# Second attention: the negated row maxima are copied into the score banks by ScalarE and VectorE in turn, where a 128-row product put them

## The chip, the cores and the metric

The kernel runs on one core of one Trainium2 chip. The metric is the device time of one execution in microseconds (us), the median of three runs. Engines are named as in the profile: PE is TensorE, PEld its weight loads, DVE is VectorE, ACT is ScalarE, POOL is GpSimd.

## The reference

The input `x` has 2048 rows of width 128. Four blocks follow one another, each on the layer-normalised output of the last and added to it: a first attention with 16 heads of width 64, a feed-forward block, a second attention, and the same feed-forward block again. The change is in the second attention. It has 8 heads of width 128, rotary positions and a causal mask:

```python
q = jnp.einsum('btm,mhd->bthd', x, w_aq)
k = jnp.einsum('btm,mhd->bthd', x, w_ak)
v = jnp.einsum('btm,mhd->bthd', x, w_av)
q = _rope(q)
k = _rope(k)
s = jnp.einsum('bihd,bjhd->bhij', q, k) / D_HEAD
...
s = s - jnp.asarray(INF_APPROX, x.dtype) * mask      # mask: i < j
p = jax.nn.softmax(s, axis=-1)
o = jnp.einsum('bhij,bjhd->bihd', p, v)
r = jnp.einsum('bihd,hdm->bim', o, w_ao)
```

The inputs are spread so widely that the softmax needs the maximum of each row, and products in one half-precision part are not exact enough.

## The kernel before, in words

Each engine has a program of its own, written out in order, and the engines meet only at semaphores: an instruction that waits holds back everything behind it on its engine.

**Tiles.** A head of the second attention has 4 units, one for each block of 512 queries (`qb` 0 to 3). A unit walks over the keys 128 at a time, so that `qb` has 4, 8, 12 or 16 steps, 40 in a head and 320 in all (`PLACES_B`, with the running number `g`). The last four steps of a unit lie on the diagonal, and their tiles are 512, 384, 256 and 128 queries wide (`c0` is where they begin). All units have an even number of steps, so `g` is even where the step is.

**A score tile.** Scores stand transposed, keys on the partitions and queries along the row. The two banks `SB[0]` and `SB[1]` take the tiles in turn. `scores_b(g)` (L1820) puts a tile there with four products of 128x512: minus the maximum of each query, lifted by a constant, comes first, as `row_units` times `MROW` (L1832). Then come, on the diagonal, the mask (L1835) and always K high times Q high, K low times Q high and K high times Q low (L1837 to L1839), since each operand is split into a high and a low half-precision part. ACT takes the exponential of the bank twice, in single precision into `PRB` (L911) and in half precision into `PAH` (L913); POOL subtracts the one from the other into `PAL` (L704). Two steps later (`LAG_B`) PE multiplies both parts by the values, in two halves (`pv_b`, L1859 to L1863, 12 products of about 128 columns for a full tile).

**The ring.** Everything else that PE makes goes through three banks, `RING3B`, as numbered items: PE writes an item (`ring_put`), DVE takes it (`ring_taken`), and item n may be written once item n-3 is taken (`claim`). The table `PLAN_B` says which items each step has, beside the tile and its values. A digit is a product of scores for the maxima of a later unit (`max_b`, L1773), of which DVE takes the maximum (L1094). P is a projection of Q or K for the next head (L1748 to L1750); DVE takes it in three instructions for the rotary positions (L1314 to L1316). V is a part of the next head's values; ACT copies it (L872), then DVE subtracts (L1335). T and O turn and project the output of the unit before. An r with a digit is the item "rows".

```python
PLAN_B = [
    ["2 2", "2", "2 T", "P O"],
    ["2 V", "2", "2 V", "2 2 2", "2 2", "T", "r2 3 P", "O"],
    ["3 3 3", "3", "3 3", "3", "3 3", "3 3 P T", "3", "3", "3 3", "P", "r3", "O"],
    ["0", "0 0", "P", "0", "P", "", "r0 1 T", "", "1 V", "1 P", "1", "1 1 1", "P", "", "1 V O", "r1"],
]
```

PE's order in a step is: the score tile, the first item, one half of the values product, the second item, the other half, the remaining items, with T and O always last. The last head has no items for a next one, so its P, V, 0 and 1 fall away.

**The rows item.** When the last maximum of a unit is taken, DVE makes `negmax` (L1097). PE turns it (L1540), and DVE writes it lifted and spread over four rows into `MROW` (L1116), which serves all tiles of the unit.

Of the kernel before, what the change touches and what calls it, by code (L numbers as in the profile page):

```python
# [35 lines left out]
F16 = mybir.dt.float16  # L36
I32 = mybir.dt.int32
ALU = mybir.AluOpType
# [3 lines left out]
P = 128  # L42
# [3 lines left out]
BLK = 512  # L46
# [226 lines left out]
def build(nc, x, adaptive_scale, Wq, bq, Wk, bk, Wv, bv, Wo, bo, gamma, beta,  # L273
          w_aq, w_ak, w_av, w_ao, W1, b1, W2, b2, rope_cos, rope_sin, out):
    ctx = ExitStack()
    with ctx:
# [84 lines left out]
        row_units = sb("row_units", [P, P], F16)  # L361
        MROW = sb("MROW", [P, 2, BLK], F16)
# [117 lines left out]
        def phase(n):  # L480
# [9 lines left out]
            s.pv = sem(f"pv_{n}")  # L490
            s.fourth_taken = sem(f"fourth_taken_{n}")
# [3 lines left out]
        sa, sbb = phase("a"), phase("b")  # L495

# [78 lines left out]
        def _(pool):  # L575
# [20 lines left out]
            pool.memset(MROW[:, :, :], 0.0)  # L596
            link(pool.memset(row_units[:, :], 0.0))
            pool.memset(row_units[0:BT, :], ROW_UNIT)
# [121 lines left out]
        def _(act):  # L720
# [183 lines left out]
            for g, (it, ul, step) in enumerate(PLACES_B):  # L904
# [37 lines left out]
        def _(dve):  # L942
# [147 lines left out]
            def take_max(s, bank, item, qt, c, width, chunks, last, unit):  # L1090


                dve.wait_ge(s.ring_put, item + 1)
                dve.reduce_max(maxes[:, qt, c:c + 1], bank[:, 0:width], X_AXIS).then_inc(s.ring_taken, 1)  # L1094
                if last:
                    dve.wait_ge(s.ring_taken, item + 1)
                    dve.tensor_reduce(negmax[:, :], maxes[:, :, 0:chunks], X_AXIS, ALU.max, negate=True  # L1097
                                      ).then_inc(s.max_ready, 1)
                    dve.wait_ge(s.max_ready, unit + 1)
# [281 lines left out]
            for i in range(BT):  # L1381
                n = 5 * BLOCKS + i
                take_max(sbb, RING3B[n % 3], n, i, 0, (i + 1) * P, 1, i == BT - 1, 0)
            take_rows(sbb, RING3B[ROWS_LEAD_B % 3], ROWS_LEAD_B, MROW[0:BT, 0, :], lifts_b[0:BT, 0:1])
            for i, (qt, c) in enumerate(max_items_b(1)):
                n = ROWS_LEAD_B + 1 + i
                take_max(sbb, RING3B[n % 3], n, qt, c, BLK if c < 1 else (qt + 1) * P, 2, i == 2 * BT - 1, 1)
            take_rows(sbb, RING3B[(LEAD_B - 1) % 3], LEAD_B - 1, MROW[0:BT, 1, :], lifts_b[0:BT, 0:1])
# [10 lines left out]
            for g, (it, ul, step) in enumerate(PLACES_B):  # L1399
# [7 lines left out]
                if place in (5, 6):  # L1407
                    normalise(4 * BLOCKS + place - 5, place - 5)
                if step == LAG_B and g > step:
                    normalise_b((ul - 1) % UNITS_B, g - step)  # L1410
                for n, item in ITEMS_B[g]:
                    bank = RING3B[n % 3]
                    if item[0] == "max":
# [3 lines left out]
                        take_max(sbb, bank, n, i, c, BLK if c < target else (i + 1) * P, target + 1,  # L1417
                                 item[2] == len(todo) - 1, it * UNITS_B + target_unit(ul, target))
                    elif item[0] == "rows":
                        h = head + (item[1] < qb)  # L1420
                        take_rows(sbb, bank, n, MROW[0:BT, item[1] % 2, :], lifts_b[0:BT, h:h + 1])
# [26 lines left out]
        def _(pe):  # L1448
# [87 lines left out]
            def rows(s, bank, item, unit):  # L1536

                claim(s, item)
                pe.wait_ge(s.max_ready, unit + 1)
                pe.transpose(bank[0:BT, 0:P], negmax[:, :], ident[:, :]).then_inc(s.ring_put, 1)  # L1540
# [277 lines left out]
            rows(sbb, RING3B[ROWS_LEAD_B % 3], ROWS_LEAD_B, 0)  # L1818
            pe.wait_ge(ones_set, 2)

            def scores_b(g):
# [3 lines left out]
                if step == 0:  # L1825
# [154 lines left out]
```

## Time and profile before

| what | value |
|---|---|
| median of 3 runs | 1928.9 us (1926.85 to 1929.04) |
| span of the profiled execution | 1927.3 us |
| PE busy | 1854.3 us, 96% |
| POOL busy | 1597.5 us, 83% |
| ACT busy | 1548.5 us, 80% |
| DVE busy | 1443.6 us, 75% |
| second attention, score tiles | 1277 to 1889 us |

The profiled execution is known by its span, from the first to the last instruction; the runs' times hold what lies around it too, and their median is 1.6 us above it. Busy time counts an instruction from its start to its end, and neighbours can overlap: PE's products have modelled ends. The pitch, from one start to the next, is what a product costs PE, and the timelines below show it.

### The profile page before, as it was taken

The page shows a single profiled execution, that of the slowest core. Times are in us where ns is not written, and L with a number is a line of the kernel's source. Part 1 is how long each engine was busy: PE and PEld are TensorE (multiplying, and loading weights), DVE is VectorE, ACT ScalarE, POOL GpSimd, SP SyncE. Part 2 cuts the span into 40 slices and gives each one's busy share as a digit, 9 for nine tenths or more (in the row PEclk, how much of TensorE's full clock was granted, in tenths as well). Part 3 has the DMA queues.
Part 4 walks back from the last instruction along what each step waited for, and adds up shares of the span by engine and source line. Part 5 has one row for each costly group of instructions (what it writes and reads, how often), then busy time and mean ns, then how long its engine had stood idle before and what let it go on. Part 6 is the DMA issues. An engine that isn't in the chain of part 4 may idle for free.

```text
span 1927.3 us, 55726 instructions
## 1 busy us (share of the span) xinstructions
PE 1854.3 (96%) x23471; PEld 1256.4 (65%) x23471; DVE 1443.6 (75%) x2647; ACT 1548.5 (80%) x1921; POOL 1597.5 (83%) x1025
## 2 busy tenths in 40 slices
PE   4899999999999999999999998779999999999998
PEld 3566666666666666666666665547777777767766
DVE  7798878878878878878878875566767767767652
ACT  4799999999999999999999999646666666666664
POOL 3899999999999999999999999358688787787752
PEclk8999999999999999999999999889999999999999
DMA  6101100100100100100100100100000000000000
GB/s 148 35 11 26 34 15 22 35 17 20 35 19 18 35 19 18 35 19 17 35 23 14 35 2 2 55 1 2 2 1 2 2 2 2 2 1 1 2 2 23
DMA packets 45034, 37.96 MB, mean 20 GB/s; under 512 B 8304, under 2 KB 44144, under 8 KB 44528
## 3 DMA queue, kind: packets, MB, share of 16 engines
q1 hardware_dynamic: 44304, 34.00, 7.0%
q8 instruction: 186, 3.05, 0.7%
q10 hardware_dynamic: 480, 0.39, 0.1%
q14 instruction: 64, 0.52, 0.1%
HBM read 8.15 MB, written 1.05 MB: 5 GB/s over the span
## 4 chain that ended last, share of the span: by engine, by line
PE 87%; DVE 4%; POOL 3%; issue 3%; ACT 2%; DMA 0%; SPq 0%; POOLq 0%; DVEq 0%; ACTq 0%
PE ST L1639 11%; PE ST L1640 11%; PE RING L1520 7%; PE OO L1601 6%; PE OO L1603 6%; PE OO L1600 6%; PE OO L1520 4%; PE ST L1832 3%; PE ST L1838 3%; PE ST L1837 3%; PE ST L1839 3%; POOL PBUF L704 2%; PE OO L1859 2%; PE OO L1861 2%; PE OO L1863 2%
## 5 line engine op out<-in xcount | busy, mean ns | idle before, releaser
L620 POOL TENSOR_TENSOR PAB<-PR,PAB 128x1024 f16<-128x1024 f32 x342 | 724.3, 2134 | 42.3 <-ACT PAB L799 42.2
L799 ACT ACTIVATE PAB<-ST,exp_scale 128x1024 f16<-128x1024 f32 x512 | 567.6, 1109 | 0.0
L1104 DVE TENSOR_REDUCE maxes<-RING 128x1 f32<-128x512 f32 x661 | 439.6, 684 | 122.6 <-PE RING L1520 118.2
L1600 PE MATMUL OO<-VP,PAB 128*128 128x66 f16 x4096 | 446.6, 192 | 2.9 <-POOL PAB L620 2.9
L1601 PE MATMUL OO<-VP,PAB 128*128 128x64 f16 x4096 | 447.1, 193 | 0.0
L1603 PE MATMUL OO<-VP,PAB 128*128 128x66 f16 x4096 | 445.1, 192 | 0.0
L797 ACT ACTIVATE PR<-ST,exp_scale 128x1024 f32<-128x1024 f32 x342 | 381.9, 1117 | 64.7 <-PE ST L1640 61.8
L1600 PEld LDWEIGHTS OO<-VP,PAB 128*128 128x128 f16 x4096 | 380.2, 96 | 78.3 <-issue 15.5
L1601 PEld LDWEIGHTS OO<-VP,PAB 128*128 128x128 f16 x4096 | 377.0, 97 | 60.6
L1639 PE MATMUL ST<-QL,KH 128*128 128x512 f16 x1024 | 388.6, 380 | 2.0 <-DVE QH L1116 1.0
L1640 PE MATMUL ST<-QH,KL 128*128 128x512 f16 x1024 | 388.8, 380 | 0.0
L620 POOL TENSOR_TENSOR PAB<-VF,PAB 128x1024 f16<-128x1024 f32 x170 | 362.6, 2133 | 26.9 <-ACT PAB L799 26.9
L1603 PEld LDWEIGHTS OO<-VP,PAB 128*128 128x128 f16 x4096 | 378.0, 98 | 0.0
L1104 DVE TENSOR_REDUCE maxes<-OO 128x1 f32<-128x512 f32 x363 | 248.4, 684 | 67.9 <-PE OO L1520 64.3
L704 POOL TENSOR_TENSOR PBUF<-PR,PBUF 128x512 f16<-128x512 f32 (+1 forms) x214 | 216.0, 1013 | 98.8 <-ACT PBUF L913 92.8
L911 ACT ACTIVATE PR<-ST,exp_scale_b 128x512 f32<-128x512 f32 (+1 forms) x214 | 133.5, 624 | 136.2 <-PE ST L1839 132.1
L1520 PE MATMUL RING<-KH,QL 128*128 128x512 f16 x661 | 228.5, 381 | 6.5 <-DMA QH<-HS 3.1
L797 ACT ACTIVATE VF<-ST,exp_scale 128x1024 f32<-128x1024 f32 x170 | 189.7, 1116 | 33.8 <-PE ST L1640 32.1
L913 ACT ACTIVATE PBUF<-ST,exp_scale_b 128x512 f16<-128x512 f32 (+1 forms) x320 | 198.1, 619 | 0.0
L1094 DVE TENSOR_REDUCE maxes<-RING 128x1 f32<-128x512 f32 (+3 forms) x216 | 128.9, 611 | 54.7 <-PE RING L1773 53.6
L1859 PE MATMUL OO<-PAB,PBUF 128*128 128x130 f16 x768 | 150.9, 220 | 2.8 <-POOL PBUF L704 2.7
L1861 PE MATMUL OO<-PAB,PBUF 128*128 128x128 f16 x768 | 151.2, 221 | 0.0
(319 smaller groups left out, 4027.8 us busy)
## 6 DMA issues: line engine op xcount, KB each, us to landing
KH<-HS SPq DMA_DIRECT2D x124, 64.0 KB, 2.0
QL<-HS SPq DMA_DIRECT2D x64, 64.0 KB, 2.0
QL<-LS SPq DMA_DIRECT2D x64, 64.0 KB, 2.0
QH<-HS SPq DMA_DIRECT2D x64, 64.0 KB, 2.0
KL<-LS SPq DMA_DIRECT2D x62, 64.0 KB, 2.0
X<-in_L_attn_a_x SPq DMA_DIRECT2D x4, 256.0 KB, 4.2
SHARED<-in_rope_cos SPq DMA_DIRECT2D x1, 1024.0 KB, 5.2
SHARED<-in_rope_sin SPq DMA_DIRECT2D x1, 1024.0 KB, 7.3
```

The costliest lines, as they stand in the source:

```text
L620: pool.tensor_tensor(PB[:, s, :], PRA[g % PR_SLOTS], PA[:, s, :], ALU.subtract).then_inc(p_low_ready, 1)
L704: pool.tensor_tensor(PAL[:, g % SLOTS_B, c0:BLK], PRB[g % PR_SLOTS_B][:, c0:BLK], PAH[:, g % SLOTS_B, c0:BLK], ALU.subtract).then_inc(p_lo ...
L797: act.activation(PRA[g % PR_SLOTS], ST[step % 2][:, :], ACT.Exp, scale=scale)
L799: act.activation(PA[:, step % SLOTS_A, :], ST[step % 2][:, :], ACT.Exp, scale=scale).then_inc(sa.exps, 1)
L913: act.activation(PAH[:, g % SLOTS_B, c0:BLK], SB[g % 2][:, c0:BLK], ACT.Exp, scale=scale).then_inc(sbb.exps, 1)
L1104: dve.reduce_max(maxes[:, i // BLOCKS, i % BLOCKS:i % BLOCKS + 1], bank[:, :], X_AXIS).then_inc(sa.ring_taken, 1)
L1520: pe.matmul(RING3[item % 3][:, :], QL16[head % 2][:, at:at + P], KH16[head % 2][:, c * BLK:(c + 1) * BLK], start=True, stop=True).then_inc ...
L1600: pe.matmul(o, high, v[:, 0:V2_AT], start=(m == 0 and qt == 0), stop=False, skip_group_check=True)
L1601: pe.matmul(o[:, V1_AT:V2_AT], high, v[:, V2_AT:VCOL], start=False, stop=False, skip_group_check=True)
L1603: ins = pe.matmul(o, low, v[:, 0:V2_AT], start=False, stop=(m == TILES - 1), skip_group_check=True)
L1639: pe.matmul(tile, KH16[hs][:, keys], QL16[hs][:, q], start=True, stop=False)
L1640: ins = pe.matmul(tile, KL16[hs][:, keys], QH16[hs][:, q], start=False, stop=True)
```

## The change

`row_units`, `MROW` and the product L1832 go. In their place:

- Behind `negmax`, DVE makes `negmax16` (lifted, scaled, half precision), 128x4.
- The rows item is now `seed_b`: four products of 128x128 (`spread`) put minus the maxima, repeated over all partitions, into a ring bank. DVE copies the whole bank into `SEED`, 128x512 in single precision (`take_seed_b`). `SEED` has two places, by the parity of `qb`.
- Before PE writes a score tile, the seed is copied from `SEED` into its bank, and PE's products add to it (none of them starts the sum). For even tiles ACT copies, behind its two instructions of tile g, the seed of tile g+2. For odd tiles DVE copies, in step g (even), the seed of tile g+1: behind the take of the step's first ring item, before the second.
- ACT's half-precision instruction no longer takes the exponential of the bank: it copies `PRB`, and waits for the first to be finished. The bank is free after the first exponential.
- Tiles 0 and 1 get their seed by `spread` straight into the bank.

```diff
 # ScalarE
-                act.activation(PRB[g % PR_SLOTS_B][:, c0:BLK], SB[g % 2][:, c0:BLK], ACT.Exp, scale=scale)
+                p = PRB[g % PR_SLOTS_B][:, c0:BLK]
+                act.activation(p, SB[g % 2][:, c0:BLK], ACT.Exp, scale=scale).then_inc(sbb.first_exps, 1)
                 wait(act, sbb.pv, g - SLOTS_B + 1)
-                act.activation(PAH[:, g % SLOTS_B, c0:BLK], SB[g % 2][:, c0:BLK], ACT.Exp, scale=scale
-                               ).then_inc(sbb.exps, 1)
+                act.wait_ge(sbb.first_exps, g + 1)
+                act.activation(PAH[:, g % SLOTS_B, c0:BLK], p, ACT.Copy).then_inc(sbb.exps, 1)
+                if g % 2 == 0 and g + 2 < len(PLACES_B):
+                    tile, seed, taken = seed_of(g + 2)
+                    act.wait_ge(sbb.ring_taken, taken)
+                    act.activation(tile, seed, ACT.Copy).then_inc(sbb.seeds_act, 1)
 # VectorE
+                    link(dve.tensor_reduce(negmax[:, :], maxes[:, :, 0:chunks], X_AXIS, ALU.max, negate=True))
+                    dve.tensor_scalar(negmax16[:, :], negmax[:, :], lifts_b[:, head:head + 1], 1.0 / ROW_UNIT,
+                                      ALU.add, ALU.mult).then_inc(sbb.max_ready, 1)
...
+            def take_seed_b(bank, item, unit):
+
+                dve.wait_ge(sbb.ring_put, item + 1)
+                dve.tensor_copy(SEED[:, unit % 2, :], bank[:, :]).then_inc(sbb.ring_taken, 1)
+
+            def seed_scores(t):
+
+                tile, seed, taken = seed_of(t)
+                dve.wait_ge(sbb.first_exps, t - 1)
+                dve.wait_ge(sbb.ring_taken, taken)
+                dve.tensor_copy(tile, seed).then_inc(sbb.seeds_dve, 1)
...
+                seeds_next = g and g % 2 == 0 and g + 1 < len(PLACES_B)
...
-                for n, item in ITEMS_B[g]:
+                for place, (n, item) in enumerate(ITEMS_B[g]):
                     bank = RING3B[n % 3]
+                    if place == 1 and seeds_next:
+                        seed_scores(g + 1)
...
+                if seeds_next and len(ITEMS_B[g]) < 2:
+                    seed_scores(g + 1)
 # TensorE
+            def spread(bank):
+
+                for i in range(BT):
+                    ins = pe.matmul(bank[:, i * P:(i + 1) * P], negmax16[:, i:i + 1].broadcast_to((P, P)),
+                                    mask_ident[:, :], start=(i == 0), stop=True, skip_group_check=True)
+                return ins
...
-                if step == 0:
-                    pe.wait_ge(sbb.ring_taken, ROWS_OF_B[it * UNITS_B + ul] + 1)
-                wait(pe, sbb.exps, g - 1)
+                if g < 2:
+                    spread(SB[g])
+                else:
+                    pe.wait_ge((sbb.seeds_act, sbb.seeds_dve)[g % 2], g // 2)
...
-                pe.matmul(tile, row_units[:, :], MROW[:, qb % 2, c0:BLK], start=True, stop=False,
-                          skip_group_check=True)
```

The first place is VectorE's order before, in the fifth head, last unit, steps 2 to 6. F and PR are the targets of a projection's take, maxes those of a maximum's:

```order
L1327 TENSOR_TENSOR AB<-OO,rden 128x384
L1314 TENSOR_TENSOR F<-RING,SHARED 128x512 [waits operands_ready_b,ring_put_b]
L1315 TENSOR_TENSOR PR<-RING,SHARED 64x512
L1316 TENSOR_TENSOR PR<-RING,SHARED 64x512
L1094 TENSOR_REDUCE maxes<-RING 128x1 [waits ring_put_b]
L1097 TENSOR_REDUCE negmax<-maxes 128x4 [waits ring_taken_b]
L1314 TENSOR_TENSOR F<-ST,SHARED 128x512 [waits operands_ready_b,ring_put_b,max_ready_b]
L1315 TENSOR_TENSOR PR<-ST,SHARED 64x512
L1316 TENSOR_TENSOR PR<-ST,SHARED 64x512
L1116 SCALAR_TENSOR_TENSOR MROW<-RING,lifts_b,rowmask 4x512 [waits ring_put_b]
```

The same place after the change, with ST<-SEED for a seed that is copied into a score bank:

```order
L1340 TENSOR_TENSOR F<-RING,SHARED 128x512 [waits operands_ready_b,ring_put_b]
L1341 TENSOR_TENSOR PR<-RING,SHARED 64x512
L1342 TENSOR_TENSOR PR<-RING,SHARED 64x512
L1125 COPY ST<-SEED 128x512 [waits ring_taken_b,first_exps_b]
L1106 TENSOR_REDUCE maxes<-RING 128x1 [waits ring_put_b]
L1110 TENSOR_REDUCE negmax<-maxes 128x4 [waits ring_taken_b]
L1111 TENSOR_SCALAR negmax<-negmax,lifts_b 128x4 [waits chain]
L1340 TENSOR_TENSOR F<-ST,SHARED 128x512 [waits operands_ready_b,ring_put_b,max_ready_b]
L1341 TENSOR_TENSOR PR<-ST,SHARED 64x512
L1342 TENSOR_TENSOR PR<-ST,SHARED 64x512
L1125 COPY ST<-SEED 128x512 [waits ring_taken_b,first_exps_b]
L1118 COPY SEED<-RING 128x512 [waits ring_put_b]
```

A seed copy now stands behind each of the two projections' takes of the even steps 2 and 4; `MROW` has become the copy of a whole bank.

The second place is TensorE's order before, in the same unit, from the last values product of step 4 into step 5. ST<-MROW opens the score tile:

```order
L1863 MATMUL ST<-PAB,PBUF 128x130
L1832 MATMUL ST<-MROW,row_units 128x512 [waits exps_b]
L1837 MATMUL ST<-QH_0,KH_0 128x512
L1838 MATMUL ST<-QH_0,KL_0 128x512
L1839 MATMUL ST<-QL_0,KH_0 128x512
L1859 MATMUL OO<-PAB,PBUF 128x130 [waits p_low_ready_b]
```

And after the change:

```order
L1899 MATMUL ST<-PAB,PBUF 128x130
L1873 MATMUL ST<-QH_0,KH_0 128x512 [waits seeds_dve_b]
L1874 MATMUL ST<-QH_0,KL_0 128x512
L1875 MATMUL ST<-QL_0,KH_0 128x512
L1895 MATMUL OO<-PAB,PBUF 128x130 [waits p_low_ready_b]
```

The tile has one product less, and its first one waits for VectorE's seed copy in place of ScalarE's exponentials of two tiles earlier.

## Rows read from the trace of the kernel before

**Rows 1.** Stretches: us; PE, PEld, DVE, ACT, POOL busy (count); granted clock; DMA.

```profile
1588.00:1664.00 76.00, 75.73 (x765) 54.49 (x764) 54.62 (x101) 51.29 (x94) 60.01 (x60) 1.00 0.01 2
1816.00:1890.00 74.00, 70.06 (x689) 49.90 (x686) 36.11 (x96) 50.07 (x87) 43.05 (x44) 0.98 0.01 2
1250.00:1270.00 20.00, 15.44 (x117) 9.96 (x116) 13.70 (x31) 8.75 (x18) 14.55 (x13) 1.00 0.00 1
1270.00:1276.00 6.00, 2.89 (x26) 1.44 (x23) 3.65 (x8) 3.40 (x5) 4.41 (x5) 0.77 0.00 0
```

**Rows 2.** Waits in the fifth head: us in total, times, longest.

```profile
ACT PR L911 <- PE ST L1839: 15.8, 18, 1.8
...
PE OO L1859 <- POOL PBUF L704: 0.3, 1, 0.3
```

**Rows 3.** Timeline, TensorE, last unit, steps 4 to 6: start, length, instruction.

```profile
1639.73 0.38 PE L1832 MATMUL ST<-MROW,row_units 128*128 128x512 f16 x1
1639.94 0.38 PE L1837 MATMUL ST<-QH,KH 128*128 128x512 f16 x1
...
1641.03 0.38 PE L1750 MATMUL ST<-XNT,WHB 128*128 128x512 f16 x1
1641.24 0.22 PE L1859 MATMUL OO<-PAB,PBUF 128*128 128x130 f16 x1
...
1641.93 0.38 PE L1832 MATMUL ST<-MROW,row_units 128*128 128x512 f16 x1
...
1644.33 0.27 PE L1540 MATMUL RING<-ident,negmax 128*4 128x128 f32 x1
1644.44 0.22 PE L1859 MATMUL OO<-PAB,PBUF 128*128 128x130 f16 x1
```

**Rows 4.** Timeline, VectorE, the last instruction of that projection's take.

```profile
1642.91 0.68 DVE L1316 TENSOR_TENSOR PR<-ST,SHARED 64x512 f32<-64x512 f32 x1
```

**Rows 5.** Timeline, TensorE, third unit, steps 4 to 7.

```profile
1618.13 0.38 PE L1773 MATMUL ST<-KH,QH 128*128 128x512 f16 x1
...
1619.25 0.38 PE L1832 MATMUL ST<-MROW,row_units 128*128 128x512 f16 x1
...
1624.07 0.38 PE L1832 MATMUL ST<-MROW,row_units 128*128 128x512 f16 x1
```

**Rows 6.** Timeline, VectorE, the same steps.

```profile
1618.55 0.69 DVE L1094 TENSOR_REDUCE maxes<-ST 128x1 f32<-128x512 f32 x1 [1.34 <-PE ST L1773]
1619.16 0.68 DVE L1094 TENSOR_REDUCE maxes<-RING 128x1 f32<-128x512 f32 x1
...
1624.86 0.68 DVE L1094 TENSOR_REDUCE maxes<-ST 128x1 f32<-128x512 f32 x1
```

**Rows 7.** Timeline, a claim that VectorE's take ends, at the first tiles.

```profile
1280.52 0.69 DVE L1094 TENSOR_REDUCE maxes<-RING 128x1 f32<-128x512 f32 x1 [3.68 <-PE RING L1773]
...
1281.27 0.10 PEld L1772 LDWEIGHTS RING<-later_keys,mask_ident 128*128 128x128 f16 x1 [0.79 <-DVE maxes L1094]
```

**Rows 8.** VectorE by line and shape: count, busy us, mean ns, idle before.

```profile
L1274 DVE TENSOR_TENSOR X<-X,XN 128x512 f32<-128x512 f32 x4 | 4.1, 1023 | 2.5 <-POOL XN L659 2.5
L1397 DVE COPY XNT<-RING 128x512 f32<-128x512 f32 x1 | 0.7, 692 | 1.1 <-PE RING L1873 1.1
L998 DVE TENSOR_SCALAR mask_ident<-ident 128x128 f16<-128x128 f32 x1 | 0.2, 220 | 0.0
L1097 DVE TENSOR_REDUCE negmax<-maxes 128x4 f32<-128x4 f32 x8 | 1.3, 158 | 0.3
```

**Rows 9.** ScalarE by line and shape.

```profile
L911 ACT ACTIVATE PR<-ST,exp_scale_b 128x512 f32<-128x512 f32 x150 | 103.2, 688 | 104.0 <-PE ST L1839 101.0 <-POOL PBUF L704 2.2
L866 ACT ACTIVATE KH<-F 128x512 f16<-128x512 f32 x30 | 18.9, 628 | 0.7 <-POOL F L681 0.6
L732 ACT ACTIVATE XNT<-OO 128x512 f32<-128x512 f32 x4 | 2.3, 584 | 2.3 <-PE OO L1452 2.3
```

**Rows 10.** GpSimd by line and shape.

```profile
L704 POOL TENSOR_TENSOR PBUF<-PR,PBUF 128x512 f16<-128x512 f32 x150 | 173.4, 1158 | 81.6 <-ACT PBUF L913 78.0 <-PE ST L1863 2.7
```

More of the change, by code:

```diff
@@ L360, in build @@
         later_keys_t = sb("later_keys_t", [P, P], F16)
-        row_units = sb("row_units", [P, P], F16)
-        MROW = sb("MROW", [P, 2, BLK], F16)
+        negmax16 = sb("negmax16", [P, BT], F16)
+        SEED = sb("SEED", [P, 2, BLK])
         wqk_raw = RAW[:, 0:HA * P].rearrange("p (h c) -> p h c", c=P)
@@ L490, in phase @@
             s.pv = sem(f"pv_{n}")
+            s.seeds_act = sem(f"seeds_act_{n}")
+            s.seeds_dve = sem(f"seeds_dve_{n}")
+            s.first_exps = sem(f"first_exps_{n}")
             s.fourth_taken = sem(f"fourth_taken_{n}")
@@ L495, in build, with seed_of @@
         sa, sbb = phase("a"), phase("b")
+        def seed_of(t):
+            it, ul, step = PLACES_B[t]
+            qb = ul % BLOCKS
+            c0 = max(0, step - BT * qb) * P
+            return SB[t % 2][:, c0:BLK], SEED[:, qb % 2, c0:BLK], ROWS_OF_B[it * UNITS_B + ul] + 1
         def wait(eng, s, value):
@@ L595, in _ @@
                                fill=1.0 / ROW_UNIT, base=0, pattern=[[-1, BT], [0, P]], channel_multiplier=1).then_inc(consts, 1)
-            pool.memset(MROW[:, :, :], 0.0)
-            link(pool.memset(row_units[:, :], 0.0))
-            pool.memset(row_units[0:BT, :], ROW_UNIT)
             pool.wait_ge(zeros_set, 1)
@@ L1416, in _ @@
                         i, c = todo[item[2]]
-                        take_max(sbb, bank, n, i, c, BLK if c < target else (i + 1) * P, target + 1,
+                        take_max_b(bank, n, i, c, BLK if c < target else (i + 1) * P, target + 1,
                                  item[2] == len(todo) - 1, it * UNITS_B + target_unit(ul, target))
                     elif item[0] == "rows":
-                        h = head + (item[1] < qb)
-                        take_rows(sbb, bank, n, MROW[0:BT, item[1] % 2, :], lifts_b[0:BT, h:h + 1])
+                        take_seed_b(bank, n, item[1])
                     elif item[0] == "project":
@@ L1534, in total_b, with seed_b @@
                           ).then_inc(sa.ring_put, 1)
[L1536 to L1540, printed above, removed]
+            def spread(bank):
[3 more added lines that the diff above has]
+                return ins
+            def seed_b(bank, item, unit):
+                claim(sbb, item)
+                pe.wait_ge(sbb.max_ready, unit + 1)
+                spread(bank).then_inc(sbb.ring_put, 1)
             def turned(s, bank, item, src, units_done):
@@ L1817, in _ @@
                 max_b(0, 0, i, 0, RING3B[n % 3], n, 0)
-            rows(sbb, RING3B[ROWS_LEAD_B % 3], ROWS_LEAD_B, 0)
+            seed_b(RING3B[ROWS_LEAD_B % 3], ROWS_LEAD_B, 0)
             pe.wait_ge(ones_set, 2)
@@ L1888, in ring_item_b @@
                 elif item[0] == "rows":
-                    rows(sbb, bank, n, it * UNITS_B + target_unit(ul, item[1]))
+                    seed_b(bank, n, it * UNITS_B + target_unit(ul, item[1]))
                 elif item[0] == "project":
@@ L1908, in _ @@
                         max_b(0, 1, qt, c, RING3B[n % 3], n, 0)
-                    rows(sbb, RING3B[(LEAD_B - 1) % 3], LEAD_B - 1, 1)
+                    seed_b(RING3B[(LEAD_B - 1) % 3], LEAD_B - 1, 1)
                 elif g > 1:
```

21 lines of the change are left out of this document (10 added, 11 removed).

## The prediction, made before the change was run

> **What bounds the kernel now.** I read the stretches first, for the share of each engine in one head of the second attention, then the waits there, then the timelines of PE and DVE side by side. The fifth head takes 76.0 us and PE is busy for 75.7 of them at the full clock, 2.4 GHz; POOL has 60.0, DVE 54.6 and ACT 51.3 [rows 1]. The waits agree: ACT waits for PE 18 times in front of L911 alone, while PE waits once for POOL, 0.3 us [rows 2]. So this part lasts as long as PE's products do, and the others have 16 to 25 us of slack per head. The reader is to see two more things. First, PE writes the next tile whenever it gets there: the product L1832 at 1641.93 follows the values products without a gap, though DVE is at that time still at work on the projection that PE ended at 1641.24 [rows 3], until 1642.91 + 0.68 = 1643.59 [rows 4]. Second, this is allowed because three ring banks stand between the two engines, and because nothing that a score tile needs comes from DVE in the same step.
>
> **What the change removes on PE.** A product of 512 columns costs its pitch, 1639.94 - 1639.73 = 0.215 us when read over several (the row has 0.21) [rows 3]. A head has 24 tiles off the diagonal and 16 on it with a mean of 320 columns, which together are 34 full widths: 34 x 0.215 = 7.3 us per head, 58.4 us for eight. The turn of the maxima (0.11 us, from L1540 at 1644.33 to L1859 at 1644.44 [rows 3]) becomes four products of 128 columns, 4 x 0.055 = 0.22 us, so 32 x 0.11 = 3.5 us come back. Before the first tile PE no longer waits for `MROW`: about 1 us less. PE's own work falls by 58.4 - 3.5 + 1 = 55.9 us. If the new seeds always came in time, that would be the gain.
>
> **The seeds of odd tiles: a new wait of PE for DVE.** In each even step g, DVE copies the seed of tile g+1 only behind the take of that step's first ring item, and PE reaches tile g+1 right behind step g. DVE's path starts at the item itself. For one maximum: the product starts at 1618.13, DVE at 1618.55 [rows 5, 6], 0.42 us later; its take has a pitch of 0.61 us (1618.55 to 1619.16) [rows 6]; then comes the copy, and then the way to PE, 0.06 us (a take ends at 1280.52 + 0.69 = 1281.21, PE's waiting load starts at 1281.27) [rows 7]. No row has a DVE copy from SBUF to PSUM. The nearest is the same instruction the other way, 0.692 us (L1397) [rows 8]; from below there is L998, 128 columns from SBUF to SBUF in 0.220 us against 0.158 us for 4 columns, which stretched to 512 gives 0.16 + 4 x 0.06 = 0.40 us; from above L1274 with two SBUF sources, 1.02 us [rows 8]. I take 0.69, since one side is in PSUM as in the nearest row. Copies of 384 and 128 columns I take at 0.55 and 0.28. So tile g+1 can start at 1618.55 + 0.61 + 0.69 + 0.06 = 1619.91, and PE was there at 1619.25 [rows 5]: a stall of 0.66 us, in a step that even had a second item behind the first.
>
> A rule of the Trainium skill bears on this price. "VectorE: DVE Perf Modes", section "Mode 2×_2P — use both read ports for one tensor", says that a single-source fp32 copy runs at two elements a cycle only where source and destination are in SBUF. By it the seed copy stays at the full 0.69 us, and the low end of 0.40 us doesn't come; the rows agree as far as they go, since the copy out of PSUM has the single rate and the narrow one inside SBUF looks faster.
>
> The same reading, step by step through the fifth head (end of DVE's take of the first item as the trace has it, plus copy and way, minus PE's start of the next tile), gives four classes of the 20 even steps:
> - The first item is a projection: 3 steps (units' steps qb3 2, 4, 12). Step 4: 1643.59 + 0.75 = 1644.34 against 1641.93 [rows 3, 4], 2.41 us. The others 2.36 and 2.22: 7.0 us.
> - A maximum or rows item that stands on DVE behind a projection of the step before: 3 steps (qb2 6 and 10, qb3 10). qb2 6: the take starts at 1624.86, so 1624.86 + 0.61 + 0.75 = 1626.22 against 1624.07 [rows 5, 6], 2.15 us. The others 1.5 and 1.4: 5.05 us.
> - One item alone, or little behind it: 5 steps, 0.74 to 1.0 us, together 4.4 us.
> - Two items, or items of middle length: 6 steps, 0.3 to 0.66 us, together 2.9 us. In the other 3 a V, P or O behind the first item covers the copy.
>
> Sum 19.3 us per head. These stalls add up, since each lies between an item that PE has just written and the next tile: time lost earlier moves both ends alike. DVE isn't full: 54.6 + 34/2 x 0.61 (half the tiles' widths, at the pitch of a take) = 65 us in a head that now lasts near 88. The seven heads with a next one: 7 x 19.3 = 135 us. The last head has no P, V, 0 or 1; there I count 8.5 us for its first three units and none from DVE in the last, where no item stands ahead of the copies.
>
> **The seeds of even tiles, on ACT.** ACT's two instructions per tile become 0.69 us and, behind a wait for the first to end (0.03), a copy of 0.63 us (L866), plus every second time a seed copy [rows 9]. That has no row either: 0.58 (L732, out of PSUM) to 0.69 us (L911) [rows 9], I take 0.6. From the tile's last product to PE's start of tile g+2 it is 0.48 + 0.72 + 0.52 + 0.6 + 0.06 = 2.4 us (0.52 is L866's pitch, its length less the tenth by which neighbours overlap). PE has, from there, one pitch, two values products of 12 x 0.057 = 0.68 us each (1641.24 to 1641.93 [rows 3]), a tile of 3 x 0.215 and its items: 2.2 us, items and the stall by DVE still to be added. So nothing in the first seven heads. In the last unit of the last head, which has hardly any items, ACT's pair of tiles takes 2 x 1.24 + 0.6 = 3.1 us against PE's 2 x (0.645 + 0.68) = 2.65: about 0.45 us for each of 6 or 7 pairs, 3 us. ACT's total, 51.3 us per head, rises to about 65. POOL's 1.16 us per tile [rows 10] is unchanged and was waited for only once [rows 2]; the stalls give it more room. `negmax16` is an instruction of four columns, below 0.4 us, a step or more ahead of its use. On the page "ScalarE: Activation LUTs", section "Step-by-step: what each stage is for", the Trainium skill says that ScalarE writes PSUM sooner than SBUF. No row here has ACT writing PSUM; by that page the seed copy would lie under L866's 0.63 us, and the sum wouldn't move, as ACT isn't what PE waits for.
>
> **Sum.** -58.4 + 3.5 - 1 + 135 + 8.5 + 3 = +90.6 us on the profiled execution's span of 1927.3, 2017.9 us; the runs' median lies 1.6 us above that span, so 2020 us.
>
> **Rivals.**
> - A, the other side: the seeds come in time and PE keeps its lead. It needs DVE to be through with item and copy before PE has done 0.215 + 0.68 us of work. For it: 21 us of slack on DVE [rows 1], and three ring banks that hide its lag today. Against it: slack is no help here, since even an idle DVE needs 1.78 us from the item on (0.42 + 0.61 + 0.69 + 0.06). It would win where take and copy together were under half a microsecond. Time: 1928.9 - 55.9 = 1873 us; with a third of the stalls left, still 1921.
> - B: the copy into PSUM is fast, 0.40 us. Every DVE-bound stall of 17 per head shrinks by up to 0.29 us: 7 x 4.6 + 2.5 = 35 us less, 1985 us. Still slower.
> - C: the stalls bring the clock down. PE would be busy 69 of 88 us, 78%. For it: 0.77 of the clock in a stretch where PE was busy for 2.9 of 6 us. Against it: full clock over 20 us with 15.4 busy, 77% [rows 1]. If it fell to 1.2 GHz for a tenth of the eight heads, some 70 us, PE's 55 us of work there would take twice as long at most: up to +40 us beside the stalls it fills, 2050 us.
> - D: late V items. ACT copies a V now behind its seed copy, 0.7 us later, and DVE waits for it in order: half a microsecond in one or two steps per head, +5 us, inside the range.
>
> **How the numbers follow.** Forecast (with D) 0.62, B 0.15, C 0.14, A 0.09, of which a third would end near no change. The range reaches down past B, with one microsecond per head of error on top, to 1965, and up to C with a slower copy, 2060. Its own range for the forecast alone is 1995 to 2045. A measurement of this kernel tells 0.2% (4 us) from no change. Faster 0.06, within 0.2% 0.03, slower 0.91.
>
> **What the profile after would show.** Right: PE idle ahead of L1873 by DVE's L1125, about 17 times a head, 2.4 us behind a projection that opens an even step, 0.6 to 1 us behind a maximum; a head of 86 to 90 us, the last one about 80; L1125 at 0.69 us; PE's busy time in the tiles some 55 us lower; hardly a wait of L1873 for ACT's seeds before the last unit. Wrong: waits of L1873 under 0.3 us (A), copies at 0.4 (B), a granted clock under 0.95 in the heads (C), or waits for ACT's seeds that are as long in sum as those for DVE, which would mean that ACT's chain, not DVE's, sets the tile.

## The result and the profile after

| | before | after |
|---|---|---|
| median | 1927.9 us (1926.2 to 1929.0) | 2064.4 us (2058.6 to 2066.5) |
| span of the profiled execution | 1927.3 us | 2061.0 us |
| first to last score tile | 1277.0 to 1887.4 us | 1274.9 to 2020.6 us |
| fifth head, start to start | 76.0 us | 95.6 us |

The change makes the kernel slower: ratio 1.0705, 95% interval 1.0693 to 1.0718. The forecast was 2020 us with a range up to 2060. The direction and the mechanism of the stalls were right; the time lies above the range, and a part of the loss that the sum had put at nothing is in it.

The page of the kernel after: busy time, the chain by engine, and TensorE's costliest group with a wait (busy, mean ns of one | idle before it):

```profile
PE 1847.9 (90%) x23255; PEld 1242.6 (60%) x23255; DVE 1543.9 (75%) x2838; ACT 1634.5 (79%) x2080; POOL 1600.8 (78%) x1022
...
PE 72%; DVE 17%; issue 5%; ACT 4%; POOL 2%; DMA 0%; SPq 0%; DVEq 0%; ACTq 0%; POOLq 0%
...
L1873 PE MATMUL ST<-QH,KH 128*128 128x512 f16 (+1 forms) x320 | 117.1, 366 | 105.0 <-DVE ST L1125 101.5
```

The busy share of PE hides the loss, since a product at half clock counts as busy for longer. The wait in the group's last column is what to look for. The waits of the fifth head (us in total, times, longest), which answer to [rows 2]:

```profile
ACT PR L919 <- PE ST L1875: 19.3, 18, 3.2
PEld ST L1873 <- DVE ST L1125: 15.4, 11, 2.6
PE ST L1873 <- DVE ST L1125: 13.4, 10, 2.4
...
PEld ST L1871 <- DVE ST L1125: 6.4, 7, 2.3
```

The same head asked for TensorE alone, for the tiles that open with the mask:

```profile
PE ST L1871 <- DVE ST L1125: 5.0, 6, 2.1
```

So PE waits 16 times for VectorE's seed in a head in which it waited once before, for POOL. The two seed copies themselves (shortest, median and longest in ns, first and last start), VectorE's and then ScalarE's:

```profile
L1125 DVE COPY ST<-SEED x159: 282/683/695, 1286.0 to 2020.3; 128x512 f32<-128x512 f32 x96, 128x128 f32<-128x128 f32 x32, 128x384 f32<-128x384 f32 x31
```

```profile
L926 ACT ACTIVATE ST<-SEED x159: 368/583/602, 1277.7 to 2016.4; 128x512 f32<-128x512 f32 x127, 128x256 f32<-128x256 f32 x32
```

**A stall.** TensorE in the fourth head (last unit, step 4 into 5, then step 6: the steps of the orders shown with the change, one head earlier). Its last product before the first of these rows started at 1623.23:

```profile
1625.69 0.39 PE L1873 MATMUL ST<-QH,KH 128*128 128x512 f16 x1 [2.24 <-DVE ST L1125]
1625.92 0.44 PE L1874 MATMUL ST<-QH,KL 128*128 128x512 f16 x1
1626.15 0.63 PE L1875 MATMUL ST<-QL,KH 128*128 128x512 f16 x1
...
1627.87 0.63 PE L1873 MATMUL ST<-QH,KH 128*128 128x512 f16 x1
1628.30 0.63 PE L1874 MATMUL ST<-QH,KL 128*128 128x512 f16 x1
```

VectorE over the same stall:

```profile
1622.82 0.69 DVE L1340 TENSOR_TENSOR F<-RING,SHARED 128x512 f32<-128x512 f32 x1 [2.51 <-PE RING L1787]
1623.52 0.69 DVE L1341 TENSOR_TENSOR PR<-RING,SHARED 64x512 f32<-64x512 f32 x1
1624.22 0.68 DVE L1342 TENSOR_TENSOR PR<-RING,SHARED 64x512 f32<-64x512 f32 x1
1624.94 0.69 DVE L1125 COPY ST<-SEED 128x512 f32<-128x512 f32 x1
```

The copy of the seed ends at 1625.63 and PE starts 0.06 us later, as in [rows 7]. VectorE had nothing to do before 1622.82: it was the order on the engine, not its load, that made PE wait 2.24 us.

**The clock.** The second pair of PE's rows starts 1628.30 - 1627.87 = 0.43 us apart where [rows 3] have 0.21: half the rate. Stretches of the kernel after (columns as in [rows 1]; the granted clock is the third number from the end):

```profile
1618.00:1620.00 2.00, 1.97 (x18) 1.50 (x19) 0.81 (x2) 0.96 (x2) 0.54 (x1) 0.82 0.00 0
1620.00:1622.00 2.00, 2.00 (x7) 0.71 (x5) 0.27 (x2) 0.82 (x2) 1.57 (x2) 0.50 0.00 0
1622.00:1624.00 2.00, 1.45 (x14) 0.91 (x12) 1.17 (x2) 1.34 (x3) 1.79 (x2) 0.83 0.00 0
1624.00:1626.00 2.00, 0.31 (x2) 0.20 (x3) 1.59 (x3) 0.00 (x0) 0.18 (x1) 1.00 0.00 0
1626.00:1628.00 2.00, 2.00 (x16) 1.59 (x15) 0.00 (x0) 1.02 (x2) 0.00 (x0) 0.52 0.00 0
```

```profile
1557.11:1652.72 95.61, 77.07 (x739) 53.83 (x737) 67.19 (x125) 62.33 (x114) 60.75 (x60) 0.95 0.01 1
1652.72:1748.36 95.64, 77.08 (x739) 53.80 (x737) 67.19 (x125) 62.24 (x114) 60.77 (x60) 0.95 0.01 1
```

A granted clock of 0.50 is the lower level, 1.2 GHz. In this head it falls three times, from 1598.8, 1619.3 and 1626.1 us on, for some 3 us each time, and each time less than 1.3 us behind the end of a wait of 2.4 to 2.6 us (from the start of PE's last product to that of the next tile). The last two falls belong to waits that follow each other within 8 us. The first one stands alone, since the next wait of this length is almost 20 us off:

```profile
1599.00:1602.00 3.00, 3.00 (x18) 2.01 (x17) 0.69 (x1) 1.32 (x2) 1.05 (x2) 0.50 0.00 0
```

Two more waits of 2.3 and 2.6 us in the same head bring no fall, and the second and third heads, with the same stalls, have one fall each. Of the eight heads, the first three have a mean clock of 0.967, 0.982 and 0.982, the next four 0.946, and what there is of the last 0.937.

### The profile page after: what moved, and what is told of

Its sections match the earlier page's. It is cut to its first block, busy times and chain, and to the rows that moved or that the text cites. A ratio compares the mean times of both kernels' runs of the same rounds, so it can differ in the third digit from the quotient of the medians.

```text
span 2061.0 us, 56077 instructions
## 1 busy us (share of the span) xinstructions
PE 1847.9 (90%) x23255; PEld 1242.6 (60%) x23255; DVE 1543.9 (75%) x2838; ACT 1634.5 (79%) x2080; POOL 1600.8 (78%) x1022
## 4 chain that ended last, share of the span: by engine, by line
PE 72%; DVE 17%; issue 5%; ACT 4%; POOL 2%; DMA 0%; SPq 0%; DVEq 0%; ACTq 0%; POOLq 0%
PE ST L1676 10%; PE ST L1677 10%; PE RING L1550 7%; PE OO L1638 6%; PE OO L1640 6%; PE OO L1637 6%; PE OO L1550 4%; DVE maxes L1106 3%; DVE ST L1125 3%; PE ST L1873 3%; PE ST L1875 2%; PE ST L1874 2%; DVE PR L1342 2%; DVE PR L1341 2%; POOL PBUF L711 1%
## 5 line engine op out<-in xcount | busy, mean ns | idle before, releaser
L1637 PEld LDWEIGHTS OO<-VP,PAB 128*128 128x128 f16 x4096 | 380.6, 96 | 78.5 <-issue 15.6
L1873 PE MATMUL ST<-QH,KH 128*128 128x512 f16 (+1 forms) x320 | 117.1, 366 | 105.0 <-DVE ST L1125 101.5
L711 POOL TENSOR_TENSOR PBUF<-PBUF 128x512 f16<-128x512 f32 (+1 forms) x106 | 107.2, 1011 | 98.0 <-ACT PBUF L922 94.6
L1895 PE MATMUL OO<-PAB,PBUF 128*128 128x130 f16 x768 | 156.0, 225 | 0.7 <-POOL PBUF L711 0.5
```

The costliest lines, as they stand in the source:

```text
L711: pool.tensor_tensor(PAL[:, g % SLOTS_B, c0:BLK], PRB[g % PR_SLOTS_B][:, c0:BLK], PAH[:, g % SLOTS_B, c0:BLK], ALU.subtract).then_inc(p_lo ...
L1637: pe.matmul(o, high, v[:, 0:V2_AT], start=(m == 0 and qt == 0), stop=False, skip_group_check=True)
```

## The experiments

Numbers "per head" are read from the trace: the time from PE's last product to its next tile, less what stands there in the kernel before, summed over the tiles that VectorE seeds.

**e1: the order on VectorE.** The seed copy stands ahead of the step's first item in all steps.

```diff
+                if seeds_next:
+                    seed_scores(g + 1)
                 for place, (n, item) in enumerate(ITEMS_B[g]):
                     bank = RING3B[n % 3]
-                    if place == 1 and seeds_next:
-                        seed_scores(g + 1)
...
-                if seeds_next and len(ITEMS_B[g]) < 2:
-                    seed_scores(g + 1)
```

> The changed kernel, with DVE's seed copy of tile g+1 moved ahead of the take of step g's first ring item. Theory (the stall is the path item, take, copy, PE): the copy is then done more than a microsecond before PE needs it, the 21 us of stalls in a head vanish, and with them the clock's loss behind them; PE is the bound again, 1875 to 1895 us, clock 0.985 or more. Rival (DVE and ACT, near 65 of 69 us busy in a head, can't follow PE any more, wherever the copy stands): stalls only change their place, 1925 us or more.

Measured: 1947.2 us (1945.8 to 1948.8), ratio to before 1.01 (1.0085 to 1.0116). The time is 52 us above the theory's band and inside the rival's; each idea holds a part of it. The same copies at the same price cost 117 us less. The stretch of one head, and its longest wait in sum (this kernel is two lines shorter there, so that L1871 is K high times Q high, which was L1873 above):

```profile
1588.00:1666.00 78.00, 71.66 (x736) 50.90 (x736) 65.31 (x124) 61.45 (x113) 59.83 (x60) 1.00 0.01 2
```

```profile
PE ST L1871 <- DVE ST L1125: 5.1, 6, 1.9
```

Stalls fall from 21.4 to 7.55 us per head, and the clock is back at full. Of these, 6.87 us stand in front of seven tiles (2.07 and 1.75 us the longest), where VectorE still works on items of steps before when the seed's turn comes. So two thirds of the stalls came from the place behind the item, one third from VectorE's queue.

**e2: what the clock costs.** The kernel after, with products by zero weights behind the last values product of the six even steps before the longest stalls, in the first seven heads; they add nothing to the output's sums, and PE works where it would stand.

```diff
+FILLS = {(2, 6): 38, (2, 10): 23, (3, 2): 40, (3, 4): 40, (3, 10): 39, (3, 12): 36}
...
+                for _ in range(count):
+                    pe.matmul(bank[:, 0:V2B_AT], zeros16[:, :], v[:, 0:V2B_AT], start=False, stop=False,
+                              skip_group_check=True)
```

> The changed kernel, with 23 to 40 products of 130 columns and zero weights put on PE ahead of the wait in the six steps per head whose stall is 1.5 us or longer, in the first seven heads; they fit into the stalls. Theory (a part of the loss is the granted clock, which falls behind long stalls): stalls end where they did, the clock of the heads rises from about 0.95 to 0.99 or more, and the time falls by some 25 to 35 us to 2030 to 2040 us. Rival (the clock costs nothing beside the stalls, what the sum lacks is all longer waits): 2064 us or more, since the added products can only lengthen PE's work.

Measured: 2040.8 us (2039.8 to 2042.9), ratio 1.059 (1.0572 to 1.0607), 1 us above the theory's band and 23.6 us below the kernel after though PE has more to do; by the spans 2061.0 - 2037.9 = 23.1 us.

```profile
1550.00:1641.00 91.00, 84.49 (x954) 63.38 (x953) 67.63 (x124) 62.22 (x113) 60.54 (x59) 1.00 0.01 2
```

From the second to the sixth, every head takes 91.0 us at a clock of 1.00; without the filling it is 92.3 at 0.982 (two heads) and 95.6 at 0.946. This shows rival C, with its size: 1.3 us in two heads and 4.6 in those at 0.946. The seven filled heads give 21.9 of the 23.1 us. The last head isn't filled and is 2.1 us shorter all the same, at a clock of 0.978 in place of 0.937; its clock differs from execution to execution. The run also shows that the stalls alone, at full clock, make a head of 91 us where the forecast had 76.0 - 7.3 + 0.4 + 19.3 = 88.4.

**e3: ScalarE's half of the change by itself.** The kernel before, but the half-precision part is a copy of the first exponential, and PE may write the bank after the first.

```diff
+                act.activation(p, SB[g % 2][:, c0:BLK], ACT.Exp, scale=scale).then_inc(sbb.first_exps, 1)
...
+                act.wait_ge(sbb.first_exps, g + 1)
+                act.activation(PAH[:, g % SLOTS_B, c0:BLK], p, ACT.Copy).then_inc(sbb.exps, 1)
...
-                wait(pe, sbb.exps, g - 1)
+                wait(pe, sbb.first_exps, g - 1)
```

> The kernel before, with only ACT's part of the change: the half-precision tile is a copy of the first exponential, and PE waits for the first exponential alone before it writes the bank again. Theory (this part is free): 1928 us within 4. Rival (the wait of ACT for itself lengthens the chain tile, ACT, POOL, values product, which PE already waits for at times): 1935 to 1950 us.

Measured: 1929.1 us (1926.8 to 1931.4), ratio 1.0007 (0.9998 to 1.0017). No difference can be told, which clears this part of the change.

**e4: all seeds on ScalarE.** VectorE copies none; ScalarE copies one behind every tile.

```diff
-                if g % 2 == 0 and g + 2 < len(PLACES_B):
+                if g + 2 < len(PLACES_B):
...
-                seeds_next = g and g % 2 == 0 and g + 1 < len(PLACES_B)
+                seeds_next = False
...
-                    pe.wait_ge((sbb.seeds_act, sbb.seeds_dve)[g % 2], g // 2)
+                    pe.wait_ge(sbb.seeds_act, g - 1)
```

> The changed kernel, with the seeds of odd tiles copied by ACT as well, behind its two instructions of the tile two before; DVE copies none. Theory (DVE's path behind the ring item makes the stalls, and ACT's own chain of 2.4 us from a tile's end to the seed two tiles on is just longer than PE's shortest way of 2.2 us): stalls of a few tenths in steps without items, ACT about 73 us busy per head, 1930 to 1960 us. Rival (any engine that copies seeds in its program's order holds PE up as DVE does): above 2000 us.

Measured: 1933.6 us (1930.4 to 1936.4), ratio 1.0028 (1.0018 to 1.0037), as the theory expected. PE's waits in a stretch of one head:

```profile
PE ST L1873 <- ACT ST L926: 1.5, 4, 0.7
...
PE OO L1895 <- POOL PBUF L711: 0.9, 3, 0.4
```

The 21 us of stalls behind VectorE are gone, so they were due to VectorE's seeds and to nothing else in the change. A head still takes 76.6 us. By the pitches of PE's products 7.6 us of it are waits: 3.4 ahead of the tiles, 1.9 ahead of the values products, 2.3 ahead of ring items. PE's work in a head is thus 69.0 us, 6.6 less than before (75.6), and it can't be had this way: 7.6 us of waits take it.

**e5: the late V.** In the kernel after, ScalarE's V copy stands ahead of its seed copy.

```diff
+                for n, item in ITEMS_B[g]:
+                    if item[0] == "values":
+                        values_high_b(1 - hs, item[1], RING3B[n % 3], n)
                 if g % 2 == 0 and g + 2 < len(PLACES_B):
...
-                for n, item in ITEMS_B[g]:
-                    if item[0] == "values":
-                        values_high_b(1 - hs, item[1], RING3B[n % 3], n)
```

> The changed kernel, with ACT's copy of a V item ahead of its seed copy of tile g+2, as the V copy stood in the kernel before. Theory (the stall of 2.4 us ahead of step 11 of the last unit is 1 us longer than forecast since DVE waits in order for the V of step 8, which ACT copies late): DVE takes that V about 0.6 us earlier, this stall falls to 1.8 us or less, the sum of stalls from 21.4 to about 20.5 us per head, and the time by 4 to 10 us. Rival (that stall is the projection of step 9 alone, whenever V comes): no change within 3 us.

Measured: 2057.0 us (2055.4 to 2060.5), ratio 1.0674 (1.066 to 1.0689), about 7 us below the kernel after, as the theory expected; the times of the two overlap by 2 us. The tile that the forecast missed most is that of the last unit's step 11. In the kernel after, VectorE stands there like this:

```profile
1636.29 0.69 DVE L1361 TENSOR_TENSOR PAB<-RING,PAB 128x512 f16<-128x512 f32 x1 [1.99 <-ACT PAB L879]
1636.89 0.68 DVE L1106 TENSOR_REDUCE maxes<-RING 128x1 f32<-128x512 f32 x1
1637.49 0.68 DVE L1340 TENSOR_TENSOR F<-ST,SHARED 128x512 f32<-128x512 f32 x1
1638.19 0.69 DVE L1341 TENSOR_TENSOR PR<-ST,SHARED 64x512 f32<-64x512 f32 x1
1638.89 0.68 DVE L1342 TENSOR_TENSOR PR<-ST,SHARED 64x512 f32<-64x512 f32 x1
1639.61 0.42 DVE L1106 TENSOR_REDUCE maxes<-RING 128x1 f32<-128x256 f32 x1
1640.07 0.69 DVE L1125 COPY ST<-SEED 128x512 f32<-128x512 f32 x1
```

ScalarE had the seed copy ahead of the V:

```profile
1635.16 0.58 ACT L926 ACTIVATE ST<-SEED 128x512 f32<-128x512 f32 x1
1635.68 0.58 ACT L879 ACTIVATE PAB<-RING 128x512 f16<-128x512 f32 x1
```

The chain of rival D works here: a V that is 0.52 us late holds VectorE, VectorE holds the seed, the seed holds PE. With the V first, the stall in front of that tile falls from 2.57 to 2.05 us, by just that pitch, and not to the 1.8 us that were expected. Over seven heads the stalls go from 149.8 to 143.7 us; the 1 us that is left of the 7 is less than the clock's own play, which differs from head to head and from execution to execution here.

**e6: the projections alone.** The seed goes ahead of the item only where that item is a projection.

```diff
+                if seeds_next and ITEMS_B[g] and ITEMS_B[g][0][1][0] == "project":
+                    seed_scores(g + 1)
+                    seeds_next = False
```

> The changed kernel, with DVE's seed copy ahead of the take only in the three steps per head whose first item is a projection. Theory (stalls add up one by one, and the clock falls where several long ones come close together): 3 x 2.4 = 7.2 us fewer stalls in each of seven heads, 50 us, and the clock's loss of some 23 us mostly gone as well: 1990 to 2000 us, stalls 14.2 us per head, clock 0.99. Rival (a stall that is taken away comes back in the next step, since DVE and ACT are what can't follow): 2030 us or more.

Measured: 1999.8 us (1998.1 to 2002.4), ratio 1.0372 (1.0356 to 1.0388), 64.6 us below the kernel after. This is inside the theory's band, though 15.1 to 15.4 us of stalls are left in a head where 14.2 were expected. In the three steps the stall falls from 2.50, 2.44 and 2.26 us to 0.38, 0.98 and 0; that is 5.8 us of the 6.1 to 6.4 that a head loses. Seven heads give 43 to 44 us. The other 21 us (17 by the spans, 2061.0 - 2000.5 = 60.5) fit the clock, which is now 1.000 or 0.980 in the heads from the second on. Heads at a clock of 1.000 take the two apart: one takes 84.8 us here and 91.0 us in e2, and these 6.2 us are the stalls; what a head of the kernel after takes beyond 91.0 us is the clock. The last head shows the clock alone, since it has no projections and the edit changes next to nothing in it: 77.4 us at 1.000 here and in e5, 78.9 at 0.978 in e2, 81.0 at 0.937 in the kernel after.

**e7 and e8: odd tiles by TensorE.** ScalarE keeps the even tiles. The odd ones get the seed by `spread`, four products of 128 columns straight into the bank (0.22 us for a full tile, as much as the product that was removed). e8 also has the V first.

```diff
...
+                elif g % 2:
+                    pe.wait_ge(sbb.first_exps, g - 1)
+                    spread(SB[1], it * UNITS_B + ul, max(0, step - BT * qb))
                 else:
-                    pe.wait_ge((sbb.seeds_act, sbb.seeds_dve)[g % 2], g // 2)
+                    pe.wait_ge(sbb.seeds_act, g // 2)
```

> Even tiles seeded by ACT as in the changed kernel, odd tiles by PE itself: the four products of 128 columns (minus the maxima in half precision, kept for three units) straight into the bank, at the price of the old product; DVE copies no seeds into score banks. Theory (DVE's path makes the stalls, ACT's seeds of even tiles cost next to nothing): half of the old product's time is saved, 29 us less 3.5 for the turned maxima, and some microseconds are lost to ACT in the last head: 1900 to 1912 us. Rival (ACT, 16 us more busy per head, holds PE up in its own right as soon as DVE doesn't): 1920 us or more.

> The same, with ACT's copy of a V item ahead of its seed copy. Theory (with PE never waiting for DVE's seeds, a later V is covered by the ring's three banks, but DVE and so a claim may wait for it): 0 to 4 us less than without. Rival (the seed copy is now the more urgent of the two): 1 to 4 us more.

Measured: 1919.0 us (1917.4 to 1920.4), ratio 0.9956 (0.9943 to 0.9968), and 1916.9 us (1916.7 to 1920.9), ratio 0.9951 (0.9939 to 0.9964). Both beat the kernel before; e7 misses the 1900 to 1912 us of its theory and ends 1 us below its rival's 1920. The 2 us between the two are no gain of the V's place: a head takes 74.9 us in both, and in the trace of e8 the first score tile starts 1.7 us sooner, which the edit can't reach. In the trace of e7:

```profile
1575.00:1650.00 75.00, 74.06 (x802) 54.64 (x801) 57.10 (x106) 61.22 (x114) 60.34 (x60) 1.00 0.01 2
```

```profile
PE OO L1899 <- POOL PBUF L711: 0.5, 2, 0.3
PE ST L1811 <- DVE PAB L1361: 0.2, 1, 0.2
PE ST L1877 <- ACT ST L926: 0.2, 1, 0.2
```

A head takes 74.9 us, 1.1 less than before. PE's own work fell by 3.2 (75.6 to 72.4, the head less the waits that the pitches show), and its waits rose from 0.4 to 2.5: the longest part, 1.3 us, ahead of the values products, for POOL's low parts. The waits listed above are shorter than the pitches' sum, since idle time counts only from a product's modelled end.

**e9 and e10: each seed where it costs least.** VectorE's copy ahead of the items as in e1, but the seven tiles with e1's longest stalls get their seed by `spread`. e10 also has the V first.

```diff
+SPREAD_B = ((1, 3), (2, 1), (2, 3), (2, 7), (2, 11), (3, 1), (3, 11))
...
+                elif g % 2 and not spread_b(g):
+                    pe.wait_ge(sbb.seeds_dve, sum(not spread_b(t) for t in range(3, g + 1, 2)))
...
```

> Even tiles as after the change. Of the odd tiles 13 per head get their seed from VectorE, copied ahead of the step's first item as in e1; the other seven, in front of which e1 still stood 6.87 us per head, get it from four products of 128 columns on TensorE, as in e7 (the turned maxima are kept for three units). Theory (what was left in e1 was VectorE's queue at those seven places, and nothing else stands behind it): a head of 78.5 - 6.87 + 6 x 0.22 + 0.06 = 73.0 us, over eight heads about 42 us less than e1: 1905 us (1900 to 1911). Rival (the wait only moves: with the seven gone, TensorE comes sooner to the ring's claims and to POOL's low parts, as in e7, where a head lost about 2 us that way): a head of 74.5 to 75.5 us, 1914 to 1922 us, with TensorE's waits for VectorE's takes and POOL in place of those for seeds.

> e9 with the V copy of ScalarE ahead of its seed copy. In e8 this brought 2 us against e7. Theory (VectorE's queue is what is waited for, and a late V holds it): 2 to 6 us less than e9. Rival (the V's place is of no account once the longest waits are gone): within 1 us of e9.

Measured: 1917.9 us (1915.2 to 1918.2), ratio 0.9944 (0.9932 to 0.9957), and 1912.4 us (1911.8 to 1914.9), ratio 0.9923 (0.991 to 0.9937). The rival of e9 holds: a head is 74.5 us. Its waits for VectorE's seeds are down to 0.4 us, as the theory had it, and PE's work is 70.3 us; but 4.15 us of waits stand in other places, 2.0 of them for POOL:

```profile
PE OO L1906 <- POOL PBUF L718: 1.0, 4, 0.3
PE RING L1574 <- DVE negmax L1118: 0.3, 1, 0.3
PE ST L1884 <- ACT ST L933: 0.2, 1, 0.2
```

e10 is 5.5 us faster than e9 by the medians, inside the theory's band, but not all of this is the V's place. By the traces (5.9 us between the spans) a head is 0.3 us shorter, 2.3 us for seven, the last head 1.0 us, with a higher clock (0.976 after 0.952), and 2.6 us lie ahead of the first score tile, which the edit can't reach; that tile starts anywhere from 1273.5 to 1278.3 us in the traces here. e10 is the fastest of all the kernels here.

| kernel | head, us | PE's work | PE's waits |
|---|---|---|---|
| before | 76.0 | 75.6 | 0.4 |
| e7 | 74.9 | 72.4 | 2.5 |
| e9 | 74.5 | 70.3 | 4.2 |
| e10 | 74.2 | 70.3 | 3.8 |
| e4 | 76.6 | 69.0 | 7.6 |
| e1 | 78.5 | 68.9 | 9.6 |

The head is the fifth of each kernel. The less PE has to do, the more it waits. No kernel came below 74 us. That the other engines' answering times set this floor is argued from these waits, and no run isolates it.

## Why the prediction was wrong in size and right in kind

The span grew by 133.7 us where the sum had 90.6.

| step | forecast | measured |
|---|---|---|
| PE's work | -55.9 | -53 to -54, by the work of e4 and e1 (6.6 to 6.7 per head) |
| stalls by VectorE's seeds, seven heads | +135 | +149.8 (21.15 to 21.50 each) |
| the same, last head | +8.5 | +13.1 |
| ScalarE in the last head | +3 | +1.0 |
| clock | 0 | +23.1 (e2) |

These measured parts give +133 to +134. They meet the span more closely than they are known: another reading of PE's pitches shifts the work by 2 us, and the 23.1 us are the difference of two single executions, in which the first score tile starts 1.2 us apart and the last head's clock differs without any filling.

- **What is removed, right.** The work of a head falls by nearly as much as the 34 widths say, less what the turned maxima cost (7.3 - 0.4 = 6.9 us).
- **The price of the seed copies, right.** VectorE's take 0.683 us where 0.69 was taken; rival B, 0.40 us, falls. ScalarE's 0.583 us against 0.6. The rule of the Trainium skill that stood beside the price (page "VectorE: DVE Perf Modes", section "Mode 2×_2P — use both read ports for one tensor": a single rate where one side is in PSUM) agrees with the 0.683 us. Only `negmax16`, which the forecast had below 0.4 us, takes 0.53 us in the median and up to 1.25; PE waited for it twice, 3.3 us in all.
- **The three projections, right:** 7.2 us against 7.0, and e6 shows that they are those steps.
- **Items behind a projection of the step before, mis-sized:** 6.4 us against 5.05. 2.35, 1.49 and 2.57 us stand against 2.15, 1.5 and 1.4. Nearly all of it is the last one, where the late V of rival D works through VectorE into the seed; e5 takes 0.52 us of that back. The other 0.65 us are three removed products, 3 x 0.215. The forecast took VectorE's end and PE's start from the same trace of the kernel before, and left out that PE gets sooner to the next tile where VectorE does not. The fifth head before, PE at tiles 8 and 11 and VectorE at its take in step 10:

```profile
1647.33 0.38 PE L1832 MATMUL ST<-MROW,row_units 128*128 128x512 f16 x1
1653.77 0.38 PE L1832 MATMUL ST<-MROW,row_units 128*128 128x512 f16 x1
```

```profile
1654.05 0.42 DVE L1094 TENSOR_REDUCE maxes<-RING 128x1 f32<-128x256 f32 x1
```

And tiles 8 and 11 in the fourth head after:

```profile
1632.45 0.38 PE L1873 MATMUL ST<-QH,KH 128*128 128x512 f16 x1
1640.82 0.39 PE L1873 MATMUL ST<-QH,KH 128*128 128x512 f16 x1 [2.40 <-DVE ST L1125]
```

From the start of tile 8, PE reached tile 11 after 6.44 us before; after the change it is there after 5.8 us (8.37 less the stall of 2.57). VectorE begins its take of step 10 at 6.72 us before, at 7.16 after (1639.61 in the rows under e5), and at 6.64 with the V first. So e5 gives VectorE the old time back, and what is left, 2.05 - 1.4 = 0.65 us, is PE's earlier arrival. The 0.20 us of the first place are the one product that its tile 6 has lost.
- **The other steps, slightly mis-sized:** 7.9 us against 7.3.
- **The last head, wrong in one point.** Its first three units give 8.9 us against 8.5. In the last unit the forecast has none, "where no item stands ahead of the copies", and there are 4.2. T and O stand there, and what VectorE does for them is ahead of the copy, as the plan shows: 2.8 us. The other 1.4 us are at the unit's start, where VectorE takes the O of the unit before and normalises its output ahead of the copies. The place of T:

```profile
2002.77 0.75 DVE L1153 TENSOR_SCALAR AT<-RING,b_down 128x512 f32<-128x512 f32 x1 [4.50 <-PE RING L1584]
2003.44 0.68 DVE L1125 COPY ST<-SEED 128x512 f32<-128x512 f32 x1
```

```profile
2004.18 0.61 PE L1873 MATMUL ST<-QH,KH 128*128 128x512 f16 x1 [1.45 <-DVE ST L1125]
```

- **The clock, the step that failed.** Rival C was held apart with 0.14 and stood outside the sum, on the strength of a stretch with 77% busy at full clock [rows 1]. A head of the kernel after has PE busy for 77.1 of 95.6 us, 81%, and the clock falls. The share was the wrong thing to compare. The forecast's own list had stalls of 2.4, 2.4, 1.4 and 2.2 us within one unit. The stretch at full clock has one wait of that length (2.3 us between the starts of two products, ended at 1258.6); the next row of [rows 1], with 0.77, falls behind waits of 1.4 and 2.0 us. So the trace of the kernel before had waits of this length with and without a fall, as the kernel after has, and could not price the clock at nothing. Forecast and C weren't alternatives: the stalls of the one bring the other, and the prediction's own sign of C, a granted clock under 0.95, came in four of the heads (0.946), beside heads of 92.3 to 95.6 us in place of 86 to 90. With 23 us added to it the forecast would have been 2043 us, and with the stalls' true size on top the measured time.
- **Rival A falls:** with the copy first (e1) it still needs 7.55 us per head.
- Of ScalarE's seeds the forecast was right: PE waits for them twice, 3.2 us in all, against 139 us for VectorE's. The longer of the two (2.9 us, in the last head) stands where the kernel before had a wait of nearly this length too, so that only 1.0 us of them is new.

On falling clocks, the Trainium skill's page "TensorE: Matmul & The Clock Gate" has two sections that point in different directions. "HAM oscillation — how this bites in real kernels" ties the fall to single idle gaps that are longer than any here; by it rival C would not have come, and the 0.50 of the trace goes against it. "A second HAM failure mode: psum-queue depth-cycling" says that frequent short idle times between groups of products can do it as well, and the stretches above agree with that one in so far as all gaps are short. Whether it is their frequency that counts no run here shows: the fall at 1598.8 us stands behind a single long wait.

## What to carry to other kernels

Taking work off the engine that is the bound did not pay here where what replaced it put another engine's answer time into its path: copies of 0.69 us, queued behind takes that wait for PE itself, cost 21 us per head while that engine was idle 30% of the time. Put the copy that is waited for ahead of what has slack, and look for what is still queued before it; but ask also what the other engines can bear, since most of a gain can turn into short waits (e7 and e9). And where a forecast lists stalls of 2 us and more on TensorE, the loss of clock belongs into the sum, with a bound, and not beside it. Where two times are read from the trace of the kernel before, ask of each how the change itself moves it.

## What the runs showed of the hardware that was not expected

- Waits of TensorE of 2.4 to 2.6 us bring the granted clock from 1.00 to 0.50 for some 3 us at a time (from 1598.8, 1619.3 and 1626.1 us on in the fourth head), with PE busy for 81% of the head, but not each of them does; filling six waits per head with products by zero keeps it at 1.00 from the second to the seventh head.
- The loss varies from head to head with nearly the same stalls. In e5, one head has 20.6 us of stalls, a clock of 0.981 and takes 91.5 us; the next has 20.2 us, 0.929 and 96.0 us. The seven full heads of the kernel after have nearly the same stalls and clocks from 0.946 to 0.982.
- ScalarE copies 128x512 in single precision from SBUF to PSUM in 0.583 us, about as long as out of PSUM (0.584 [rows 9]), and less than SBUF to SBUF (0.628 [rows 9], where the output is half precision, so that the place isn't the only difference).
